# Ten instead of eight key tiles of each head on VectorE in an attention kernel with a mixture-of-experts layer

## The reference

```
Q, K, V = heads of x@Wq+bq, x@Wk+bk, x@Wv+bv
for w in 16 wavelengths:
    m = cos(phase_modulators)[w]                    # one factor per head
    s = (Q*m) @ (K*m)^T / sqrt(8);  s = s*cos(2.7e-12 * s*s)
    acc += softmax(s) @ V * interference_weights[w]
x = layernorm(x + (acc/16) @ Wo + bo)
probs = softmax(x @ router_w + router_b)            # 8 experts and an identity
h = gelu(x @ w1[e]);  y = h @ w2[e]                 # all 8 experts, 128 -> 512 -> 128
x = layernorm(x + sum over the two best experts of gate * y, + gate_identity * x)
```

## Time and profile before

| | us |
|---|---|
| median of 3 runs | 7051.27 (7050.78 to 7051.92) |
| the profiled execution | 7051.52 |
| its span | 7049.8 |
| ACT busy | 6863.3 (97%) |
| PE busy | 6037.2 (86%) |
| DVE busy | 5561.3 (79%) |
| Pool busy | 90.1 (1%) |

### The profile page before, as it was taken

How to read it: one execution, slowest core, us unless ns; L and a number is a source line. 1 busy time by engine, 2 the same in 40 slices (tenths; PEclk the granted TensorE clock), 3 DMA queues, 4 the chain that set the end, 5 groups by cost and what they waited for, 6 DMA issues and landing times.

```text
span 7049.8 us, 123440 instructions
## 1 busy us (share of the span) xinstructions
PE 6037.2 (86%) x47044; PEld 2280.3 (32%) x47044; DVE 5561.3 (79%) x7479; ACT 6863.3 (97%) x1202; POOL 90.1 (1%) x244
## 2 busy tenths in 40 slices
PE   7888888888888888888888888888888888888888
PEld 3222222222333333333333333333333333333326
DVE  6777777777888888888878888888878788887873
ACT  6999999999999999999999999999999999999994
POOL 0000000000000000000000000000000000000000
PEclk8999999999999999999999999999999999999999
DMA  2000000000000000000000000000100000000001
GB/s 62 3 4 4 3 4 4 4 3 7 29 25 30 18 28 29 15 30 27 25 30 23 21 29 18 28 29 15 32 27 22 30 23 21 29 18 28 29 13 37
DMA packets 59007, 150.49 MB, mean 21 GB/s; under 512 B 10208, under 2 KB 26464, under 8 KB 58208
## 3 DMA queue, kind: packets, MB, share of 16 engines
q1 hardware_dynamic: 53536, 138.99, 6.3%
q10 hardware_dynamic: 4160, 2.10, 0.1%
q0 software_dynamic: 768, 1.57, 0.1%
HBM read 132.14 MB, written 10.49 MB: 20 GB/s over the span
## 4 chain that ended last, share of the span: by engine, by line
ACT 59%; issue 17%; PE 17%; ACTq 6%; DVE 1%; DMA 0%; SPq 0%; DVEq 0%
ACT ring L601 57%; PE pv L677 12%; ACTq L598 5%; ACT tile_h L614 1%; PE tr L693 1%; PE tr L1276 1%; PE sc L1266 1%; PE pv L683 1%; PE sc L653 1%; ACTq L599 1%; PE sc L634 0%; ACT L614 0%; ACTq L593 0%; PE sc L288 0%; DVE rowmax L795 0%
## 5 line engine op out<-in xcount | busy, mean ns | idle before, releaser
L601 ACT ACTIVATE ring<-scores 128x8192 f32<-128x8192 f32 (+3 forms) x1024 | 6657.1, 6612 | 39.9 <-DVE scores L805 27.1
L677 PE MATMUL pv<-ring,vh 128*32 128x512 f32 x30720 | 3963.0, 629 | 963.9 <-ACT ring L601 962.2
L677 PEld LDWEIGHTS pv<-ring,vh 128*32 128x32 f32 x30720 | 998.0, 114 | 3577.2 <-issue 2084.4
L795 DVE TENSOR_REDUCE rowmax<-sc 128x1 f32<-128x1024 f32 x512 | 601.3, 1216 | 243.8 <-PE sc L634 243.6
L805 DVE COPY scores<-sc 128x1024 f32<-128x1024 f32 (+1 forms) x512 | 601.0, 1215 | 156.5 <-PE sc L653 156.5
L834 DVE SCALAR_TENSOR_TENSOR vprobs<-ring,vprobs 128x1024 f32<-128x1024 f32 x512 | 627.2, 1225 | 17.6
L833 DVE SCALAR_TENSOR_TENSOR vprobs<-vprobs,vbits 128x1024 f32<-128x1024 f32 x512 | 627.2, 1225 | 17.6
L832 DVE SCALAR_TENSOR_TENSOR vprobs<-ring 128x1024 f32<-128x1024 f32 x512 | 623.4, 1218 | 7.2
L840 DVE COPY numer<-pv 128x512 f32<-128x512 f32 x384 | 263.5, 686 | 393.0 <-PE pv L683 379.3
L675 PE MATMUL pv<-vpower,vlast 128*32 128x512 f32 x2048 | 530.4, 593 | 0.0
L683 PE MATMUL pv<-vprobs,vlast 128*32 128x512 f32 x2048 | 529.8, 592 | 0.0
(11 more groups left out here) (160 smaller groups left out, 2596.8 us busy)
## 6 DMA issues: line engine op xcount, KB each, us to landing
tile_w<-in_L_ffn_w SPq DMA_DIRECT2D x192, 512.0 KB, 3.9
qt<-q_scratch SPq DMA_DIRECT2D x256, 36.0 KB
kt_<-k_scratch SPq DMA_DIRECT2D x256, 36.0 KB
ring<-in_L_ffn_w SPq DMA_DIRECT2D x2, 2048.0 KB, 10.8
ring<-in_L_attn_x ACTq DMA_DIRECT2D x4, 512.0 KB, 6.7
...
```

The lines of the kernel that those rows point to most:

```text
L601: nc.scalar.activation(ring[:, i % SLOTS, 0:CHUNK[i % 2]], scores[:, bass.ds(n % 2, 1), :, :].rearrange("p o k s -> p (o k s)")[:, 0:CHUNK ...
L677: last = nc.tensor.matmul(sums, vh[:, buf, kt, window], ring[:, w % SLOTS, kt * S + qh * HALF:kt * S + (qh + 1) * HALF], start=(first and ...
L795: nc.vector.tensor_reduce(rowmax[:, t:t + 1], sc[:, t % 2, :], axis=AX.X, op=ALU.max).then_inc(sc_free, 1)
```

## The change

VectorE makes the eighth key tile in ten waves of each head, 1, 3, 5, 7, 9, 11, 12, 13, 14 and 15. The blocks are numbered by their place in this list; up to block 5 the old timetable stays, and from slot 11 on there is about one block per slot. A block's buffer is `vpower` and `vprobs` of its number modulo 2, and the bits of the exponents now stand in `vprobs` itself, so `vbits` is gone; the polynomial is the same product of factors in another order of instructions. The sum over wavelengths moves from slot 1 to 3, the token tile's last layer norm from slot 13 to 15. ACT's fourth quad of waves is written out with its own sizes, and the very first wave is exponentiated in eight instructions of one key tile, each as its scores are copied. The values are stored with each head's in one piece, and Pool loads them from there with a DMA, straight into `vh`; `vv` and its loads on SP are gone.

```diff
-CHUNK = (KT * S, (KT - 1) * S)
+KEPT = (KT - 1) * S
...
+OWN_WAVES = (1, 3, 5, 7, 9, 11, 12, 13, 14, 15)
+BUFS = 2
...
-    v_dram = nc.dram_tensor("v_scratch", (B, P, KT, E), FP32, kind="Internal").ap()
+    v_dram = nc.dram_tensor("v_scratch", (B, P, H, KT, D), FP32, kind="Internal").ap()
...
-                nc.vector.tensor_tensor(vs[b].rearrange("p (t e) -> p t e", e=E), tr[:, :, :].rearrange("p a (t e) -> p (a t) e", e=E),
-                                        bv_sb.rearrange("p (o e) -> p o e", o=1).to_broadcast([P, KT, E]),
+                nc.vector.tensor_tensor(vs[b].rearrange("p (h t d) -> p t h d", t=KT, d=D), tr[:, :, :].rearrange("p a (t h d) -> p (a t) h d", h=H, d=D),
+                                        bv_sb.rearrange("p (o h d) -> p o h d", o=1, d=D).to_broadcast([P, KT, H, D]),
...
-        def put_values(pool, n, values, buf):
-            nc.gpsimd.tensor_copy(vh[:, buf, :, VAT:VAT + D], values).then_inc(vh_copied, 1)
-            pool.wait_ge(vh_copied, n + 1)
+        def put_values(pool, n, buf):
+            pool.dma_start(vh[:, buf, :, VAT:VAT + D],
+                           v_dram[bass.ds(n // H, 1), :, bass.ds(n % H, 1)].rearrange("o p i t d -> p (o i t) d")).then_inc(v_loaded, 16)
...
+            def wavelength(n, w, i, cols):
+                act.reg_load(scale[i % 2], scale_bits[:, bass.ds(w * H + n % H, 1)])
+                act.wait_ge(slot_free, W * n + w + 1)
+                apart(act)
+                nc.scalar.activation(ring[:, i % SLOTS, 0:cols],
+                                     scores[:, bass.ds(n % 2, 1), :, :].rearrange("p o k s -> p (o k s)")[:, 0:cols],
+                                     ACT.Exp, scale=scale[i % 2]).then_inc(probs_ready, 1)
+
             def quads(n, first, last):
                 with act.Fori(first, last) as quad:
+                    act.wait_ge(sc_free, USES * (n + 1))
                     for i in range(4):
-                        w, chunk = 4 * quad + i, W * n + 4 * quad + i
-                        if i == 0:
-                            act.wait_ge(sc_free, USES * (n + 1))
-                        act.reg_load(scale[i % 2], scale_bits[:, bass.ds(w * H + n % H, 1)])
-                        act.wait_ge(slot_free, chunk + 1)
+                        wavelength(n, 4 * quad + i, i, KEPT if i % 2 else KT * S)
+
+            def last_quad(n):
+                for w in range(W - 4, W):
+                    wavelength(n, w, w, KEPT if w in OWN_WAVES else KT * S)
+
+            def first_wavelength():
+                act.reg_load(scale[0], scale_bits[:, 0:1])
+                for k in range(KT):
+                    act.wait_ge(sc_free, ROW_USE + 1 + k + 1)
+                    if k == 0:
                         apart(act)
-                        nc.scalar.activation(ring[:, i % SLOTS, 0:CHUNK[i % 2]],
-                                             scores[:, bass.ds(n % 2, 1), :, :].rearrange("p o k s -> p (o k s)")[:, 0:CHUNK[i % 2]],
-                                             ACT.Exp, scale=scale[i % 2]).then_inc(probs_ready, 1)
-            with act.Fori(0, H) as n:
-                quads(n, 0, 4)
+                    last = nc.scalar.activation(ring[:, 0, k * S:(k + 1) * S], scores[:, 0, k, :], ACT.Exp, scale=scale[0])
+                last.then_inc(probs_ready, 1)
+
+            first_wavelength()
+            for w in range(1, 4):
+                wavelength(0, w, w, KEPT if w % 2 else KT * S)
+            quads(0, 1, 3)
+            last_quad(0)
+            with act.Fori(1, H) as n:
+                quads(n, 0, 3)
+                last_quad(n)
...
+        def share(n, block):
+            return VSTEPS * (len(OWN_WAVES) * n + block)
...
+            owned = w in OWN_WAVES
+            block = OWN_WAVES.index(w) if owned else 0
+            at = block % BUFS
...
-                    if kt == KT - 1 and w2 == 1:
+                    if kt == KT - 1 and owned:
                         if qh == 0:
-                            pe.wait_ge(vexp_step, VSTEPS * (8 * n + pair) + POWER_STEP)
-                        nc.tensor.matmul(sums, vlast[:, buf, 0, window], vpower[:, pair % 2, cols], start=False, stop=final)
+                            pe.wait_ge(vexp_step, share(n, block) + POWER_STEP)
+                        nc.tensor.matmul(sums, vlast[:, buf, 0, window], vpower[:, at, cols], start=False, stop=final)
...
-            if w2 == 1:
-                pe.wait_ge(vexp_step, VSTEPS * (8 * n + pair) + VSTEPS)
+            if owned:
+                pe.wait_ge(vexp_step, share(n, block) + VSTEPS)
...
+        def exponents(dve, m, block, first=False):
...
+            bits = vprobs[:, at, :].bitcast(I32)
...
-                dve.wait_ge(slot_free, SLOTS + W * m + 2 * pair - 2)
+                read = W * m + OWN_WAVES[block - BUFS] if block >= BUFS else W * (m - 1) + OWN_WAVES[block - BUFS]
+                dve.wait_ge(slot_free, SLOTS + read + 1)
...
+        def polynomials(dve, m, block):
...
-            then(nc.vector.scalar_tensor_tensor(probs, vmant, EXP2_ALPHA, vmant, ALU.add, ALU.mult))
-            then(nc.vector.scalar_tensor_tensor(probs, probs, EXP2_BETA, vbits.bitcast(FP32)[:, :], ALU.add, ALU.mult))
-            nc.vector.scalar_tensor_tensor(probs, vmant, EXP2_GAMMA, probs, ALU.add, ALU.mult).then_inc(vexp_step, 1)
+            then(nc.vector.scalar_tensor_tensor(probs, vmant, EXP2_GAMMA, probs, ALU.add, ALU.mult))
+            then(nc.vector.scalar_tensor_tensor(vmant, vmant, EXP2_ALPHA, vmant, ALU.add, ALU.mult))
+            nc.vector.scalar_tensor_tensor(probs, vmant, EXP2_BETA, probs, ALU.add, ALU.mult).then_inc(vexp_step, 1)
+
+        def blocks(dve, n, at, more):
+            if at < 11:
+                step = exponents if at % 2 else polynomials
+                step(dve, n, (at + 3) // 2)
+            elif at == 11:
+                exponents(dve, n, 7)
+                polynomials(dve, n, 7)
+            elif at == 12:
+                exponents(dve, n, 8)
+            elif at == 13:
+                polynomials(dve, n, 8)
+                exponents(dve, n, 9)
+            elif at == 14:
+                polynomials(dve, n, 9)
+                if more:
+                    exponents(dve, n + 1, 0)
+            elif more:
+                polynomials(dve, n + 1, 0)
+                exponents(dve, n + 1, 1)
...
                     normalise(dve, n - 1, NF // 2 - 1)
+                if at == 3 and carried:
                     sum_wavelengths(dve, n - 1)
...
-                pair = (at + 3) // 2
-                step = exponents if at % 2 else polynomials
-                if pair < 8:
-                    step(dve, n, pair)
-                elif more:
-                    step(dve, n + 1, pair - 8)
+                blocks(dve, n, at, more)
                 if at == 4 and part == 2:
                     tile_gates(dve, i, then)
-                if at == 13 and part == 2:
+                if at == 15 and part == 2:
                     tile_finish(dve, i, then)
```

More of the change, by code:

```diff
@@ L123, in build @@
         kt_ = sb("kt_", [P, S])
-        vv = sb("vv", [P, KT, E])
         scores = sb("scores", [P, 2, KT, S])
@@ L128, in build @@
         head_q, head_k = qt, kt_
-        vpower = sb("vpower", [P, 2, S])
-        vprobs = sb("vprobs", [P, 2, S])
-        vbits = sb("vbits", [P, S], I32)
-        vmant = ring[:, 1, CHUNK[1]:KT * S]
+        vpower = sb("vpower", [P, BUFS, S])
+        vprobs = sb("vprobs", [P, BUFS, S])
+        vmant = ring[:, 1, KEPT:KT * S]
         vlast = sb("vlast", [P, 2, 2, VW])
@@ L514, in load_weights, with tile_loads @@
                 sp.dma_start(tile_w[:, k % 2, :], cols[:, k * WC:(k + 1) * WC]).then_inc(tile_weights[k % 2], 16)
-            def tile_loads(i, ahead, values=None):
+            def tile_loads(i, ahead):
                 sp.wait_ge(tile_x1_made, i + START)
@@ L526, in tile_loads @@
                     load_head(sp, m)
-                if values is not None:
-                    sp.wait_ge(vh_ready, H * values)
-                    load_v(sp, values)
                 for k in range(4):
@@ L615, in scalar_main @@
                 act.preload_act_table(ACT.Exp)
-                quads(n + 1, 1, 4)
+                quads(n + 1, 1, 3)
+                last_quad(n + 1)
         def slot_of(use):
@@ L683, in weigh_values @@
                     last = nc.tensor.matmul(pv[g * VC:(g + 1) * VC, f % 2, :], vlast[:, buf, 1, window],
-                                            vprobs[:, pair % 2, qh * HALF:(qh + 1) * HALF], start=False, stop=final)
+                                            vprobs[:, at, qh * HALF:(qh + 1) * HALF], start=False, stop=final)
             last.then_inc(slot_free, 1)
@@ L805, in copy_scores @@
             nc.vector.tensor_copy(scores[:, bass.ds(m % 2, 1), k, :].rearrange("p o s -> p (o s)"), sc[:, use % 2, :]).then_inc(sc_free, 1)
-        def exponents(dve, m, pair, first=False):
-            base = VSTEPS * (8 * m + pair)
```

(24 more changed lines are left out.)

30 lines of the change are left out of this document (14 added, 16 removed).

## The result

| | us |
|---|---|
| before, beside it | 7051.02 (7050.45 to 7051.92) |
| after, median of 4 runs | 7261.97 (7252.25 to 7264.1) |
| ratio | 1.0296 [1.0279, 1.0314] |
| predicted | 7138 (7075 to 7185) |
| the profiled execution's span | 7262.5 (before 7049.8) |

It is 211 us slower where I had forecast 87: the sign and the places were right, the size was not, and the time lies outside my range.

A forecast was written before the change was run, and what follows sets the result against it. ACT's own instructions were taken to bound the kernel, with new waits in the pairs: - 27.5 (single heads) + 117.6 (pairs) - 6.4 (first wavelength) + 3.0 (tail) = +86.7 us on the median of 7051.3, 7138 us; range 7075 to 7185.

The forecast's parts named there:

- ACT gains 1.72 us a head, 27.5 in the single heads: Heads 0 to 15: waves 12 and 14 each lose a tile on ACT, without new waits; 16 x 1.72 = 27.5 us gained.
- 2.0 and 2.0: New ACT waits before waves 0 and 1 of the head behind a part-1 head, 2.0 us each, from PE and VectorE hand-overs.
- First wavelength, 6.4: Start of the kernel: exponentials in one-tile pieces let wave 1 begin earlier; 5.7 to 6.7 us gained, 6.4 taken.
- Layer norm in the tail, 3.0: Last head: layer norm moved to slot 15 stands between the last numer copy and the tail's first step; 3.0 us lost.
- Values by DMA, 0: Pool's copy of the values becomes a DMA issued one head (102 us) before its need; cost 0.
- The hand-over chains: In the pairs PE and VectorE hand work to each other in turn, making ACT wait before waves 0 and 1.
- 2.4: New ACT wait before wave 0 of the head behind a part-2 head, 2.4 us, from the chain after wave 13.
- the backlog's 1.6: After a part-2 head VectorE has no pause until slot 3's row maxima: ACT waits 0.2 at wave 5, 1.4 at 7.
- The step that failed: Pairs: 8.3 us of new ACT waits against 3.4 gained, 4.9 longer each, 220.0 us; 24 x 4.9 = 117.6 lost.
- rival C: Chains also catch PE at its lower clock, one wave 1.2 us late in each pair: +29, 7167 us; chance 15%.
- Rival A: ACT stays the bound, VectorE finds its 26 us a pair in idle time: 113.5 gained, 6938 us; chance 12%.
- the row to distrust: VectorE's share in a pair: busy 175.5 of 215.06 us, and the change gives it 26 more.

The follow-up runs named there:

- the run with the polynomial first: Kernel after, with VectorE making the polynomial before the hidden-layer copy or the experts' additions in slots 13 and 14 of paired heads; 7105.29 us, 1.0075.
- the run with the zeros in all stalls: Kernel after, with PE given products with a zero matrix in the pairs where it stood waiting for VectorE; 7212.76 us, 1.0229.

## Why the prediction was half right

- *ACT gains 1.72 us a head, 27.5 in the single heads*: right but for three waits of 0.28 and some 0.1 us of lost overlap at each. At the first small Exp after is 26.75 ahead (1847.07 for 1873.82), where the start and 17 heads would give 36.8: the first part-1 head stands behind it, and ACT waits 4.14 and 4.20 us in front of the next head's waves 0 and 1, where the forecast had 2.0 and 2.0.
- *First wavelength, 6.4*: 7.55 in this execution (80.33 for 87.88). One tile takes 1.06 us, inside my bounds. The start itself varies: with the same code wave 1 begins at 80.39, 81.66 and 82.53 us in the profiles of three other runs, so 5.4 to 7.6 us, and the forecast lies in that.
- *Layer norm in the tail, 3.0*: 2.99. What the sum left out there is the last head's own chain: PE waits 1.16 us for the last polynomial, and the last copy of sums starts 91.9 us behind the small Exp for 89.8, 2.1 us. *Values by DMA, 0*: no wait of PE names them, though Pool waits 3.0 us for each DMA (3.9 at most), and with all of it kept and eight tiles the time is before's.
- *The hand-over chains*: right where PE keeps its clock. 2.0 and 2.0 came as 1.98 and 1.86, 2.4 as 2.11, the backlog's 1.6 as 1.15 behind a 0.64 that is PE's break in wave 0'; too low at wave 15 (0.3 for 0.93). That the last interval's sum comes out so near to mine is in part luck, since the break is no part of the forecast. The mechanism and the places of the waits hold, and the run with the polynomial first takes most of those of slots 13 and 14 away.
- *The step that failed* is the sum of the pair: 8.3 us of new waits (8.9 with the old one), 24 x 4.9 = 117.6. Measured are 13.62, and (206.22 + 26.75) / 23 = 10.1 us a pair for 4.9. All products stood in it at the durations of a kernel in which PE never waits long. I did have the mechanism, as rival C, but as one late wave of 1.2 us; it is three places a pair: 1.8 more at 4', 1.2 at 0'', 1.6 at 1'', and 0.35 at 6, together 5.0 over the last interval. By the traces they feed on each other: a slow wave makes VectorE late, a late VectorE makes a longer stall, the stall brings the lower clock. C's chance of 15% and the edge of 7185 were too small for that. The last interval's 220.44 for 220.0 is 0.4 more of new waits, 0.6 less behind Gelu, and some 0.7 because ACT loses its 0.1 us of overlap at each of seven waits (a full exponential takes 7.04, and steps 6.93 where the next follows at once).
- *Rival A* (VectorE finds its time in idle slots) is refuted for this timetable and holds in part for another: with the two more blocks in slots 4 to 12 of the part-2 head, ten tiles go in there almost free. For part-1 heads it was not tried. That VectorE's total was the row to distrust was half the truth: it was busy 88%, and what decides is whether it has a pause between PE's hand-over and PE's next need.

By "TensorE: Matmul & The Clock Gate" of the Trainium skill, section "HAM oscillation — how this bites in real kernels", a wait that comes back with every tile puts the array back to its lower clock every time; the page's wait is for a DMA, the one here for VectorE. The trace agrees: 3.21 and 5.61 for 2.26 and 3.64 us behind the 3.53 us stall, and the maxima product takes 3.2 us behind a stall of 3.4 to 3.5 in each pair of the loop. The sum had no term for it.

What stays open: which of the near waves (8 or 9) gets the lower clock, and why in e.g. 13 of 23 pairs of one kernel and 22 of 23 of another. The runs show that it does and what it costs, not by what rule. Open is also how much of the last interval's gain is the clock's and how much comes of PE's break and VectorE's missing pause of 0.48 us by themselves; and the run with the zeros in all stalls brought back 49 us, not the 5 us a pair that I put down to the clock. Its share of the loss is read from the traces, and no run takes the lower clock away alone.
